# RWKV mixing, recurrence and SwiGLU in one kernel: chunk 1's K and V in two accumulating passes, an earlier first norm, chunk 3's scaling behind round 1's norm, and OUT arguments and weight conversions on GpSimd

## The reference

```python
xx = jnp.pad(x, ((0, 0), (1, 0), (0, 0)))[:, :-1]
xk = x * time_mix_k + xx * (1.0 - time_mix_k)      # the same for xv, xr
k = jnp.einsum('btc,dc->btd', xk, Wk)              # v with Wv; r with Wr
sr = jax.nn.sigmoid(jnp.einsum('btc,dc->btd', xr, Wr))
w = -jnp.exp(time_decay)
rwkv = sr * _wkv(w, time_first, k, v)              # a scan over time
x = _layernorm(x + jnp.einsum('btc,dc->btd', rwkv, Wo))
h = jax.nn.silu(x @ wg.T) * (x @ wu.T)             # 768 hidden, int32 weights * 1/127
x = _layernorm(x + h @ wd.T)
```

## Time and profile before

| | |
|---|---|
| median of 3 runs | 310.6 us (309.38 to 312.05) |
| the profiled execution | 310.04 us, of which the span is 308.2 us |
| granted TensorE clock over the span | 0.962 |
| PE busy | 274.2 us, 89% of the span |
| DVE busy | 273.1 us, 89% |
| ACT busy | 217.1 us, 70% |
| POOL busy | 147.9 us, 48% |

### The profile page before, as it was taken

One profiled execution on the slowest core, in us unless ns is written; L12 is line 12 of the kernel. 1 busy time (PEld: TensorE's weight loads), 2 busy tenths in 40 slices (PEclk: granted clock), 3 DMA queues, 4 the chain that ended last, 5 costly groups with the idle time before them and its releaser, 6 DMA issues.

```text
span 308.2 us, 4400 instructions
## 1 busy us (share of the span) xinstructions
PE 274.2 (89%) x1250; PEld 198.8 (64%) x1250; DVE 273.1 (89%) x484; ACT 217.1 (70%) x386; POOL 147.9 (48%) x123
## 2 busy tenths in 40 slices
PE   7588569942999999999999999999999999999991
PEld 5334456712689467955786477746793679868790
DVE  5999798726999999999999999999989999989673
ACT  3488577328976698659775888569865976399384
POOL 3556344647384727481739155743846172006030
PEclk9989599995899999999999999999999999999998
DMA  7902200031110400122022201030102002101003
GB/s 254 323 2 68 69 2 1 0 136 23 48 35 2 102 35 14 55 68 70 0 70 55 82 0 68 0 102 0 68 0 68 1 0 70 34 2 68 0 4 106
DMA packets 13523, 16.24 MB, mean 53 GB/s; under 512 B 704, under 2 KB 11200, under 8 KB 13504
## 3 DMA queue, kind: packets, MB, share of 16 engines
q1 hardware_dynamic: 12816, 15.48, 15.8%
q10 hardware_dynamic: 688, 0.53, 0.5%
HBM read 11.81 MB, written 4.19 MB: 52 GB/s over the span
## 4 chain that ended last, share of the span: by engine, by line
DVE 35%; PE 23%; ACT 20%; issue 15%; DMA 2%; DVEq 1%; POOL 1%; ACTq 0%; SPq 0%; POOLq 0%
DVE state L658 6%; PE bank_a L1026 5%; DVE stats L703 5%; PE bank_a L1003 4%; PE bank_b L1003 3%; DVE wts L629 3%; ACT x L433 3%; DVE res L716 3%; ACT act L484 3%; DVE pmax L612 2%; ACT wts L410 2%; PE bank_c L961 2%; DVE res L765 2%; PE bank_b L980 2%; DVE kv L652 2%
## 5 line engine op out<-in xcount | busy, mean ns | idle before, releaser
L347 POOL TENSOR_TENSOR hlo<-hid,hhi 128x512 fp32r<-128x512 f32 (+1 forms) x36 | 54.3, 1511 | 46.3 <-ACT hhi L492 46.2
L332 POOL TENSOR_TENSOR mix<-mix,xt 128x512 f32<-128x512 f32 x48 | 56.7, 1212 | 12.9 <-ACT mix L418 12.9
L418 ACT ACTIVATE mix<-dx,par 128x512 f32<-128x512 f32 x48 | 31.2, 711 | 25.3 <-POOL dx L326 25.3
L1026 PE MATMUL bank_a<-wd_r,hhi 128*128 128x256 f32 x192 | 46.5, 285 | 0.6 <-ACT act L484 0.2
L1026 PE MATMUL bank_a<-wd_r,hlo 128*128 128x256 f32 x192 | 45.2, 278 | 0.0
L339 POOL TENSOR_TENSOR den<-wts,state 128x512 f32<-128x512 f32 x14 | 16.7, 1194 | 55.7 <-DVE state L646 55.7
L492 ACT ACTIVATE hhi<-hid 128x512 fp32r<-128x512 f32 (+1 forms) x54 | 31.1, 578 | 12.4 <-DVE hid L749 12.2
L1026 PEld LDWEIGHTS bank_a<-wd_r,hhi 128*128 128x128 f32 x192 | 36.0, 188 | 3.6 <-issue 2.5
L1026 PEld LDWEIGHTS bank_a<-wd_r,hlo 128*128 128x128 f32 x192 | 36.0, 188 | 0.3 <-issue 0.2
L410 ACT ACTIVATE wts<-wts 128x512 f32<-128x512 f32 (+1 forms) x54 | 28.0, 578 | 8.5 <-DVE wts L629 8.5
L1003 PE MATMUL bank_a<-x1hi,wg_r 128*128 128x512 f32 (+1 forms) x96 | 32.0, 414 | 1.4 <-ACT act L484 0.9
(11 more groups left out here) (103 smaller groups left out, 548.1 us busy)
## 6 DMA issues: line engine op xcount, KB each, us to landing
xt<-xT SPq DMA_DIRECT2D x7, 513.0 KB, 3.7
xrow<-x SPq DMA_DIRECT2D x7, 512.0 KB, 3.8
out<-y SPq DMA_DIRECT2D x6, 512.0 KB, 2.8
wg_i<-wg SPq DMA_DIRECT2D x1, 768.0 KB, 8.6
wu_i<-wu SPq DMA_DIRECT2D x1, 768.0 KB, 10.1
wd_i<-wd SPq DMA_DIRECT2D x1, 768.0 KB, 11.8
out<-y SPq DMA_DIRECT2D x3, 256.0 KB, 2.1
xt<-xT SPq DMA_DIRECT2D x2, 257.0 KB, 2.9
```

What stands on the lines that cost most here:

```text
L332: nc.gpsimd.tensor_tensor(mix[:, s, i, h, 0:n], mix[:, s, i, h, 0:n], xt[:, h, 0:n], ALU.add).then_inc(mixed, 1)
L347: nc.gpsimd.tensor_tensor(hlo[:, m, 0:n], hid[:, m % NH, 0:n], hhi[:, m, 0:n].bitcast(f32), ALU.subtract).then_inc(hlo_ready, 1)
L418: nc.scalar.activation(mix[:, s, i, h, 0:n], dx[:, h, 0:n], ACT.Copy, scale=par[:, MIX + i, h:h + 1]).then_inc(dx_scaled, 1)
L1026: mm = nc.tensor.matmul(ffn[:, q, :], hp.bitcast(f32) if full else hp, w[:, m, :], start=(m == 0 and q % 2 == 0 and part is hhi), stop=(m ...
```

## The change

On PE, K and V of chunk 1 no longer wait for the mixed inputs. Since mixing is linear, `project_last_step` multiplies the weights with `xt` itself (four matmuls of 512 columns), and `project_change` adds the weights times the scaled differences, from the buffer that ACT writes (four more). POOL's mixing of K and V of chunk 1 goes away; its R is still mixed. V's first half of the first pass stands before `attention_out(0)`, the rest behind it. R of chunk 1 moves from round 0 into round 1, between the gate and up products and `down`. Six `keep_warm` matmuls before and behind the transposes go away, and the flag comes behind the transposes.

On DVE, round 0 has the residual and statistics of chunk 0 after the first running maximum, and `norm_rows` before the second `gaps`. The argument of OUT is no longer written by DVE, but by POOL in every round (`out_arg`). The conversions of wg and wu move from ACT to POOL. ACT spreads the six instructions of the range check over its early work, and splits x1 of chunk 0 before the weights of chunk 1. Chunk 1's R is scaled behind the `rstd` of chunk 0, chunk 2's V and K behind the weights of chunk 1. In round 1 only chunk 2's R is scaled before `first_norm(1)`, and all of chunk 3 behind it. The receptance of chunk 1 comes after the six silu. The load of chunk 2's `xt` waits for the V of chunk 1, since PE reads `xt` directly. POOL's loop over rounds 3 to 6 is written out.

```diff
@@ SP
+        def mixes(c):
+            return (c - 2) * (3 * CH) + CH
...
             def load_xt(c):
+                if isinstance(c, int) and c == 2:
+                    sp.wait_ge(v_ready, 2 * CH)
                 if not (isinstance(c, int) and c == 1):
-                    sp.wait_ge(mixed, (c - 1) * (3 * CH))
+                    sp.wait_ge(mixed, mixes(c))
@@ POOL
+            def out_arg(c, h):
+                pool.wait_ge(gap_ready, c * CH + (h + 1))
+                n = steps(c)
+                nc.gpsimd.tensor_scalar(wts[:, OUT, h, 0:n], gap[:, h, 0:n], par[:, FIRST, h:h + 1], CAP, ALU.add,
+                                        ALU.min).then_inc(out_arg_ready, 1)
...
-                if isinstance(j, int) and j == 1:
-                    mix_chunk(2, 0, (K, R))
+                if j == 1:
+                    mix_chunk(2, 0, [R])
                 if ahead:
                     pool.wait_ge(rwkv_ready, j + 1)
                     diffs(j + 2)
-                    mix_chunk(j + 2, s)
+                    if j > 1:
+                        mix_chunk(j + 2, s)
+                if not last(j):
+                    out_arg(j + 1, 0)
+                    out_arg(j + 1, 1)
+                if j == 1:
+                    mix_chunk(3, s)
...
-            mix_chunk(1, 1)
-            pool.wait_ge(wd_in, 16)
-            nc.gpsimd.tensor_copy(wd_r[:, :, :], wd_i[:, :, :]).then_inc(wd_ready, 1)
+            out_arg(0, 1)
+            for w_out, w_int, w_in, w_ready in ((wg_r, wg_i, wg_in, wg_ready), (wu_r, wu_i, wu_in, wu_ready),
+                                                (wd_r, wd_i, wd_in, wd_ready)):
+                pool.wait_ge(w_in, 16)
+                nc.gpsimd.tensor_copy(w_out[:, :, :], w_int[:, :, :]).then_inc(w_ready, 1)
+            mix_chunk(1, 1, [R])
+            out_arg(1, 0)
+            out_arg(1, 1)
             diffs(2)
-            mix_chunk(2, 0, [V])
+            mix_chunk(2, 0, [V, K])
@@ ACT, round_ and first_norm
-                    if m == 0:
+                    if m == 0 and not (isinstance(j, int) and j == 1):
                         receptance(j)
...
+                if isinstance(j, int) and j == 1:
+                    receptance(1)
...
                 if isinstance(j, int) and j == 1:
-                    scale_chunk(2, 0, (K, R))
+                    scale_chunk(2, 0, [R])
+                    first_norm(j, nxt)
+                    scale_chunk(3, s)
+                    return
...
                 if first(j):
-                    scale_chunk(2, 0, [V])
-                    nc.scalar.activation(wu_r[:, :, :], wu_i[:, :, :], ACT.Copy).then_inc(wu_ready, 1)
+                    scale_chunk(1, 1, [R])
+                    x1_high(0, 0)
+                    x1_high(0, 1)
+                    weights(1, 0)
+                    weights(1, 1)
+                    scale_chunk(2, 0, [V, K])
+                    return
@@ DVE, round 0 and later rounds
-                    next_max(1)
+                    carry_max(1)
+                    running_max(1, 0)
+                    norm_stats1(0)
+                    running_max(1, 1)
+                    gaps(1, 0)
+                    norm_rows(0, x1, res1, mv1, rstd1, rstd1_ready, x1_ready, halved(0))
+                    gaps(1, 1)
+                    range_flag()
                     exp_args(1, 0)
...
-                exp_args(j + 1, 1, (IN_NEW, IN_OLD))
+                exp_args(j + 1, 1)
                 x1_low(j, 0)
                 x1_low(j, 1)
-                exp_args(j + 1, 1, [OUT])
@@ PE
+            def project_last_step(i, halves=range(CH)):
+                w, bank = ((wkT, bank_a), (wvT, bank_d))[i]
+                pe.wait_ge(xt_in, 16)
+                if i == K:
+                    pe.wait_ge(gap_ready, CH)
+                else:
+                    pe.wait_ge(num_parts, 1)
+                for d in halves:
+                    for h in range(CH):
+                        nc.tensor.matmul(bank[:, d, :], w[:, h, d * P:(d + 1) * P], xt[:, h, 0:N],
+                                         start=(h == 0), stop=False)
+
+            def project_change(i):
+                w, bank, ready = ((wkT, bank_a, k_ready), (wvT, bank_d, v_ready))[i]
+                for d in range(CH):
+                    for h in range(CH):
+                        pe.wait_ge(dx_scaled, i * CH + h + 1)
+                        mm = nc.tensor.matmul(bank[:, d, :], w[:, h, d * P:(d + 1) * P], mix[:, 1, i, h, :],
+                                              start=False, stop=(h == CH - 1))
+                    mm.then_inc(ready, 1)
...
                 elif isinstance(j, int) and j == 1:
+                    project(1, 1, R)
                     down(0, range(3), full)
```

More of the change, by code:

```diff
@@ L567, in _ @@
             scale_chunk(1, 1, [K])
+            range_check(0, 0)
             weights(0, 1)
@@ L943, in project @@
                     pe.wait_ge(mixed0, before + 1)
+                elif isinstance(c, int) and c == 1:
+                    pe.wait_ge(mixed, CH)
                 else:
-                    pe.wait_ge(mixed, (c - 1) * (3 * CH) + (place(c, i) + 1) * CH)
+                    pe.wait_ge(mixed, mixes(c) + (place(c, i) + 1) * CH)
                 n = steps(c)
```

87 lines of the change are left out of this document (41 added, 46 removed).

## The result

The changed kernel takes **312.44 us** (median of 20 runs, 310.99 to 313.26), the kernel before, on the same chip, 310.10 (median of 20, 308.78 to 312.05). The ratio is 1.0071 with a 95% interval of 1.0055 to 1.0087: a loss of about two microseconds where a gain of 6.5 was forecast. The profiled execution's span is 311.1 us (308.2 before) and its mean granted clock 0.950 (0.962). POOL is busy for 181.4 us instead of 147.9, DVE for 268.9 instead of 273.1.

A forecast was written before the change was run, and what follows sets the result against it. PE and DVE were taken to bound settled rounds, and chunk 1's norm behind chunk 3's scalings in ACT's order to cause round 2's stall. -6.75 + 1.7 - 1.5 on 310.04 gave 303.5 us, range 298.5 to 308.5.

The forecast's parts named there:

- Part 1, the head: Head: rwkv(0) ends about 2.5 us sooner, and chunk 0's first silu starts at 38.8 us instead of 42.04.
- Part 2, round 1: Round 1: chunk 1's R and receptance join the chain; rwkv(1) ends at 55.5, leaving the head worth half a microsecond.
- Part 3, round 2: Round 2: earlier norm of chunk 1 brings the first hid to 76.4 from 83.15 (-6.75 us); halved clock costs +1.7.
- POOL's OUT arguments of chunk 2, the first at 68.5 with 0.8 each: Round 2: POOL's arguments follow chunk 3's differences; ACT's last exponentials of chunk 2 then end at 70.7 us.
- The gain of the scaling itself: Round 2: with chunk 3's six scalings behind chunk 1's norm, the first hid comes 6.75 us sooner.
- for the clock alone: Round 2 behind the first hid: PE runs 5 us at the halved clock after its wait, costing +1.7 us.
- Part 4, the settled rounds: Settled rounds: DVE loses two OUT writes, giving -0.25 us a round for six rounds, -1.5 us in all.
- The slower rival: Every round: POOL's OUT arguments hold DVE's IN arguments and recurrence; at 2 us per instruction 319.4 us; chance 0.06.
- The sum: Whole kernel: -6.75 + 1.7 - 1.5 = -6.55 on the profiled 310.04 gives 303.5 us.
- the waits only move: Load of `xt(2)` lands 3 us later, shifting round 1 and `xt(3)`; settled rounds give nothing; 308.2 us; chance 0.18.

The follow-up runs named there:

- the price of one argument: Changed kernel with other forms of POOL's OUT argument in chunks 4 to 6, only durations read: a second operation costs 0.45 us, the scalar per partition 0.07.
- OUT on POOL: Kernel before with OUT arguments on POOL behind each round's mixing and POOL's loop written out; 306.89 us, ratio 0.9908.
- loop: Kernel before with only POOL's loop over rounds 3 to 6 written out; 308.34 us, ratio 0.9938.
- OUT on DVE: Changed kernel with DVE writing the OUT arguments again; 308.92 us, ratio 0.9973.
- scaling: Kernel before with only chunk 3's six scalings moved behind the norm of chunk 1; 307.65 us, ratio 0.9933.
- R early: Changed kernel with chunk 1's R projected between chunk 0's hidden tiles 1 and 2, receptance behind the first silu; 309.71 us, ratio 0.9981.
- arguments first: Changed kernel with POOL's two OUT arguments of chunk 2 ahead of chunk 3's differences in round 1; 311.11 us.
- K late: Changed kernel with POOL's mixing of chunk 2's K behind the low parts of round 1; 310.47 us.
- mended: Changed kernel with OUT on DVE, chunk 1's R and receptance early, POOL's round 2 as K, V, den, four low parts, R; 307.34 us, ratio 0.9883.
- best: Kernel before with OUT on POOL except chunk 2's, loop written out, chunk 3's scaling behind the norm, round-2 R mixed after four low parts; 304.84 us, ratio 0.9801.
- interleaved: Kernel before with chunk 3's scaling behind the norm, POOL's round 2 as K, den, three low parts, V and R, three low parts; 311.25 us.
- combination: Kernel before with OUT on POOL except chunk 2's, loop written out, chunk 3's scaling behind the norm, round-2 mixing interleaved with low parts; 308.32 us.

## Why the prediction was wrong, step by step

**Part 1, the head: wrong by 3.3 us at the first silu.** rwkv(0) was to end 2.5 sooner and ends 0.9 sooner. DVE's second scan waited 1.40 us for ACT's exponentials, which stood behind a range check (12.80 to 13.72), with POOL's second OUT argument ending only at 13.8. DVE's next two scans took 3.37 us together, against 1.38 before, beside POOL's conversions of wu and wd, which I had called covered; POOL's OUT arguments had pushed these conversions back into the scans. PE's first half of V then ran at half clock (3.57 us, where its second half took 1.88). V's second pass ends at 30.9 and POOL's mixing of R at 31.4, so `xt(2)` is issued at 31.49 instead of 29.0. The load itself took 4.3 us, as I chose, but POOL's differences took 2.95 instead of 2.2. The four scalings, the table, and the silu behind them follow as worked out, 3.3 late. With OUT back on DVE the same silu is at 39.9, so 2.2 of the 3.3 go with the OUT arguments.

**Part 2, round 1: the chain was right, but it begins late.** From the start of R to the end of rwkv(1) it takes 9.6 us, and 9.4 were worked out; moving R and the receptance out of it brings rwkv(1) 4.4 forward. What I left out is POOL's queue: the mixing of K, moved ahead of the low parts, held the fourth hid by 1.50 us; putting it back brought rwkv(1) 2.1 forward, 1.3 of it behind the first hid. rwkv(1) is 4.4 later than forecast: 3.3 from the silu, and the rest mostly this wait.

**Part 3, round 2: the failing step is "POOL's OUT arguments of chunk 2, the first at 68.5 with 0.8 each".** The two took 4.15 us, 2.08 each. That is beyond my upper bound of 1.66, which was a two-input subtraction; the cast to which I held it nearer says nothing of this form. By the sum the first argument ends at 68.5 and the last exponential at 70.7, 3.0 us behind the differences; it was 4.8 (72.4 to 77.2), so this step adds 1.8 us to the first hid. The run with OUT back on DVE agrees, with 1.7. Round 1 brings 4.4, and 0.2 are left for the load (5.1 us), the differences and smaller terms; that makes the 6.4 by which the first hid is late (82.82 for 76.4). Together with the 2.2 of the head, this one price is the largest error of the forecast. The gain of the scaling itself was forecast too high by 1: in the kernel with that part alone the first hid came 5.8 sooner counted from rwkv(1), and 6.75 were forecast.

The time from the first hid of round 2 to rwkv(2), in all kernels but that of the price of one argument, with how long PE's granted clock was 0.50 in it:

| POOL's mixing of chunk 3 | from first hid to rwkv(2), us | of it at the lower clock, us |
|---|---|---|
| before the first hid (before, OUT on POOL, loop) | 12.3, 12.4, 12.1 | 0, 0, 0 |
| all of it before den, beside the hidden tiles (after, OUT on DVE, scaling, R early, arguments first, K late) | 14.7, 15.2, 15.2, 14.7, 15.0, 14.7 | 6.0, 3.5, 3.4, 3.0, 4.4, 4.3 |
| K and V before den, R last (mended, best) | 15.5, 15.6 | 6.0, 6.2 |
| interleaved (interleaved, combination) | 16.8, 16.8 | 5.9, 6.2 |

I had 1.7 us for this stage, for the clock alone; in the changed kernel it is 2.4, and in the others with the earlier norm 2.4 to 4.4. That I priced no POOL work here is the second failing step: the earlier norm moved POOL's mixing from before the first hid to beside the hidden tiles. The clock changes in the same kernels, so the table alone does not part the two. In the second line the stage is no longer where the lower clock lasted twice as long, and in each of its kernels the fourth hid comes 7.9 to 8.4 us behind the first, at the end of POOL's first low part: there POOL's queue sets the time. With less mixing ahead of the low parts that wait is gone and PE's up products set it, at the lower clock. What the stage would take at the full clock stays open; warming PE in its wait was not tried.

**Part 4, the settled rounds: forecast -0.25 a round, measured 0, and +0.1 like for like.** The rows above show the two writes paid back in full. And the written-out loop hides a little: the kernels with it and OUT on DVE have 32.86 us a round, those with it and OUT on POOL 32.96. The slower rival is refuted as a mechanism of the settled rounds, though its premise came true: it put the turning point at 1.5 us for one POOL instruction, and at 2.1 the rounds still take 32.96, because hardly anything is late by it: POOL's second argument ends at 147.0, ACT's last exponential at 147.8, and DVE's second scan comes at 148.9.

**The sum.** rwkv(2) is 7.2 us later than forecast. Round 3 adds 1.1: rwkv(2) is 2.1 behind the kernel before and rwkv(3) 3.2, and the copy of `pmax` takes 1.00 beside POOL's mixing, where it took 0.19 in this round of the kernel before. The settled rounds add 1.5. The round of chunk 7 gives back 1.2, from the loop written out, which the forecast put at nothing without a reason. That makes 8.6, against 8.4 by which rwkv(8) is late; the median is 8.9 over the forecast. The rival "the waits only move" had much of the mechanism (the load of `xt(2)` lands at 35.8 for 33.3, the chain of round 1 has no slack, the settled rounds give nothing), at 308.2, without POOL's part.

## What to carry to other kernels

When a wait of one engine goes away, list what other engines did during it: that work now runs beside something else, and may stand in a queue that others wait for. An instruction moved to another engine is priced by a row of the same form there, and without one the bound must be wide; whether the price matters is decided by who stands behind it in the queue: the same move cost 3.5 us in one order and nothing that shows in another. Before the time of an event is read as an effect, look at an event that the edit cannot touch: the same head differed by 1.3 us between traces here. A loop that hides the size of its last pass can make full-size work out of half a chunk.

## What the runs showed of the hardware

- GpSimd's `tensor_scalar` of 128x512 with two operations takes 2.14 us on average (14 of them, with VectorE at work beside them), of 128x256 1.30 (4); VectorE's takes 0.48. The Trainium skill's "GPSIMD Engine Reference", section "Engine selection", calls one-input operations roughly line-rate on GpSimd; for this form the measurement says over four times VectorE's time, and 1.7 us with one operation, and it decides.
- A VectorE copy of 128x2 takes 0.17 to 0.19 us where GpSimd is idle or the phase is good, and 0.96 to 1.09 beside a run of GpSimd's adds in the settled rounds. When those adds ended earlier (232.2 instead of 236.4), the copy at 232.5 took 0.17 where it had taken 1.06. That agrees with the exclusive lock in the Trainium skill's "SBUF — State Buffer", section "Who interferes with whom": a small instruction waits for a large one to end.
- PE's granted clock was at its lower level (0.50) behind a wait for the silu of 3.3 to 5.3 us in each kernel that has the earlier norm, for 3.0 to 6.2 us between the first hid of round 2 and rwkv(2). In the changed kernel it was there from 75.6 to 78.6 too, ahead of that wait, when PE had been busy for 8.19 of the ten microseconds from 65 to 75.
